# PSUM banks split three and five instead of four and four in a gated recurrent block

## What is computed

```python
rkv = x @ W_rkv + b_rkv ; r, k, v = split(rkv)
r = sigmoid(r) ; k = exp(k) ; kv = k * v
u1 = scan(lam, kv) ; u2 = scan(lam, k)            # y[t] = lam * y[t-1] + in[t], along the sequence
att = (u1 + gamma * kv) / (u2 + gamma * k + 1e-6) * r
z = layernorm(x + att @ W_o + b_o)
xr = mu_r * z + (1 - mu_r) * z_prev ; xk = mu_k * z + (1 - mu_k) * z_prev
out = layernorm(z + sigmoid(xr @ W_r) * (square(relu(xk @ W_k)) @ W_v))
```

## Time and profile before

| | |
|---|---|
| median of 3 runs | 2562.32 us (2560.85 to 2562.44) |
| the profiled execution | 2561.6 us, of it span 2559.8 us |
| mean granted TensorE clock | 0.992 of full speed |
| TensorE matmul busy | 2511.2 us, 98% of the span |
| VectorE, ScalarE, GpSimd busy | 79%, 50%, 48% |
| DMA | mean 43 GB/s |

### The profile page before, as it was taken

The page is one execution under the profiler, slowest core; times in us unless marked ns, Lnnn a source line. Parts: engine busy times, 40 slices in busy tenths (PEclk is TensorE's granted clock), DMA queues, the critical chain, the costliest instruction groups (busy, mean ns, idle before and its releaser), DMA issues.

```text
span 2559.8 us, 32879 instructions
## 1 busy us (share of the span) xinstructions
PE 2511.2 (98%) x11268; PEld 2076.2 (81%) x11268; DVE 2020.1 (79%) x2698; ACT 1269.4 (50%) x2159; POOL 1221.5 (48%) x1102
## 2 busy tenths in 40 slices
PE   6999999999999999999999999999999999999996
PEld 4888888888888888888888888888888888888885
DVE  8878888778787787877787887878877888777772
ACT  4444455454554444554445554545544455545454
POOL 4454454445454545544454535455444545454552
PEclk8999999999999999999999999999999999999998
DMA  4011111011100111101111111111011111111100
GB/s 160 17 50 50 33 50 34 34 51 50 34 34 35 49 50 33 50 34 34 50 50 34 38 35 45 50 35 49 34 34 50 50 35 40 36 41 50 41 30 21
DMA packets 57784, 110.63 MB, mean 43 GB/s; under 512 B 7040, under 2 KB 7040, under 8 KB 57088
## 3 DMA queue, kind: packets, MB, share of 16 engines
q1 hardware_dynamic: 57600, 108.31, 12.5%
HBM read 74.73 MB, written 33.55 MB: 42 GB/s over the span
## 4 chain that ended last, share of the span: by engine, by line
PE 96%; DVE 1%; issue 1%; ACT 1%; POOL 1%; DMA 0%; ACTq 0%; SPq 0%; POOLq 0%; DVEq 0%
PE bankB L835 13%; PE bankA L825 13%; PE bankA L827 13%; PE bankA L826 13%; PE bankB L837 13%; PE bankB L836 13%; PE bankB L877 5%; PE bankB L878 5%; PE bankB L879 5%; PE bankB L856 2%; DVE x_lo L626 0%; DVE gate L667 0%; DVE att_f L678 0%; DMA x_f<-in_xT 0%; DVE gate L670 0%
## 5 line engine op out<-in xcount | busy, mean ns | idle before, releaser
L825 PE MATMUL bankA<-x_hi,wrkv_hi 128*128 128x512 f32 x1536 | 603.2, 393 | 18.8 <-DVE x_lo L626 18.8
L827 PE MATMUL bankA<-x_hi,wrkv_lo 128*128 128x512 f32 x1536 | 599.6, 390 | 0.0
L826 PE MATMUL bankA<-x_lo,wrkv_hi 128*128 128x512 f32 x1536 | 599.5, 390 | 0.0
L670 DVE RECIPROCAL gate<-gate 128x512 f32<-128x512 f32 x128 | 429.2, 3353 | 4.4
L320 POOL TENSOR_TENSOR att_f<-att_f,gate 128x512 f32<-128x512 f32 x128 | 214.4, 1675 | 319.8 <-DVE att_f L683 319.6
L825 PEld LDWEIGHTS bankA<-x_hi,wrkv_hi 128*128 128x128 f32 x1536 | 289.5, 189 | 80.6 <-issue 16.6
L827 PEld LDWEIGHTS bankA<-x_hi,wrkv_lo 128*128 128x128 f32 x1536 | 289.4, 188 | 60.7
L826 PEld LDWEIGHTS bankA<-x_lo,wrkv_hi 128*128 128x128 f32 x1536 | 289.7, 189 | 59.1
L344 POOL TENSOR_TENSOR xk_lo<-xk_f,xk_hi 128x512 fp32r<-128x512 f32 x128 | 173.8, 1387 | 263.8 <-ACT xk_hi L491 263.8
L348 POOL TENSOR_TENSOR xr_lo<-xr_f,xr_hi 128x1024 fp32r<-128x1024 f32 x64 | 179.4, 2804 | 225.3 <-ACT xr_hi L495 225.3
L329 POOL TENSOR_TENSOR ve<-mv,eps_ln 128x2 f32<-128x2 f32 x128 | 60.9, 476 | 458.9 <-DVE mv L696 455.1
(11 more groups left out here) (89 smaller groups left out, 5431.1 us busy)
## 6 DMA issues: line engine op xcount, KB each, us to landing
x_f<-in_xT SPq DMA_DIRECT2D x128, 256.0 KB, 4.0
y<-in_x SPq DMA_DIRECT2D x128, 256.0 KB, 2.7
out<-z SPq DMA_DIRECT2D x128, 256.0 KB, 2.1
wrkv_f<-in_w_rkv SPq DMA_DIRECT2D x3, 768.0 KB, 6.8
wo_f<-in_w_o SPq DMA_DIRECT2D x1, 1024.0 KB, 10.3
wr_f<-in_w_r SPq DMA_DIRECT2D x1, 1024.0 KB, 12.0
wk_f<-in_w_k SPq DMA_DIRECT2D x1, 1024.0 KB, 13.9
wv_f<-in_w_v SPq DMA_DIRECT2D x1, 1024.0 KB, 15.9
```

The source lines that it names most:

```text
L670: dve.reciprocal(gate[:, c % 2], gate[:, c % 2]).then_inc(rec_made, 1)
L825: pe.matmul(bank[:], w_hi, x_hi[:, h], start=(h == 0), stop=False)
L826: pe.matmul(bank[:], w_hi, x_lo[:, h], start=False, stop=False)
L827: last = pe.matmul(bank[:], w_lo, x_hi[:, h], start=False, stop=(h == NC - 1))
```

## The change

Three banks go to the projections and five to the other products. Projection n now uses `bankA[n % 3]`, so each of K, V and R has a bank of its own, and waits on what took projection n-3: the one of its own kind in the chunk before. Slot n of the other products uses `bankB[n % 5]` and waits on what took slot n-5. At the start of step 0 TensorE writes five `bankB` instead of four, one more matmul, and `begin_sum` waits for five there.

```diff
-NBANK = 4
+NA, NB = 3, 5
 ...
-            return bankB[slot_of(name, index) % NBANK]
+            return bankB[slot_of(name, index) % NB]
 ...
-            n = slot_of(name, index) - NBANK
+            n = slot_of(name, index) - NB
 ...
-                act.activation(key[:, c % 2], bankA[(3 * c) % NBANK][:], ACT.Exp, bias=b_sb[:, 0, c:c + 1])\
+                act.activation(key[:, c % 2], bankA[(3 * c) % NA][:], ACT.Exp, bias=b_sb[:, 0, c:c + 1])\
 ...
-                        dve.wait_ge(columns_written, NBANK)
+                        dve.wait_ge(columns_written, NB)
 ...
-                m = n - NBANK
+                m = n - NA
 ...
-                bank = bankA[n % NBANK]
+                bank = bankA[n % NA]
 ...
-                            pe.matmul(bankB[h][:], wrkv_hi[:, c, which, h], x_hi[:, h], start=True, stop=True)\
-                                .then_inc(columns_written, 1)
+                            for bank_b in (bankB[h:h + 1] if h < NC - 1 else bankB[h:]):
+                                pe.matmul(bank_b[:], wrkv_hi[:, c, which, h], x_hi[:, h], start=True, stop=True)\
+                                    .then_inc(columns_written, 1)
```

## The result

Slower. The median of four runs is 2590.53 us (2588.63 to 2591.35) against 2562.36 us before; the ratio is 1.0112 with a 95% interval of 1.0100 to 1.0124, so 28 us more. The forecast was 24.5 us more, 2586 us in a range from 2581 to 2591. The ratio times the median before is 2591.1 us: the result sits on the range's upper edge, by this figure just past it. Direction and place were right, the size was 4 us short.

A forecast was written before the change was run, and what follows sets the result against it. TensorE, full in the steady steps, was taken to bound the kernel. 24.3 us for K3's wait plus 0.2 us for step 0, on 2561.6 us, gave 2586 us, range 2581 to 2591.

The forecast's parts named there:

- TensorE is full, and each tenth is paid 31 times: Steady steps: matmuls and transposes fill 78.0 of 78.10 us, so each new tenth of waiting is paid 31 times.
- K3 and only K3 waits in the steady steps: Of twelve projections only K3 lacks room: `exp_key` 2 frees its bank 0.79 to 0.87 us late, mean 0.845.
- The term of 24.3 us: K3's wait in 31 steps: 0.845 + 0.05 signal delay - 0.11 made up = 0.785 us a step.
- Step 0, 0.2 us: Start of step 0: the fifth bank costs one more matmul, 0.23 us, counted as 0.2 us.
- V2's wait in step 0: In step 0 TensorE stands 2.3 us at V2 until V1 is taken; counted as nothing because covered.
- the very thing that was to cover step 0: TensorE's 15.6 us wait at step 0's end for VectorE's low parts, said to cover V2's and V3's waits.
- The last block, 0 us: Last block: the 0.7 us receptance wait goes, but the value products wait 1.9 + 0.7 us instead; gain 0.
- The rival with the clock: K3's wait makes the clock fall, about 1.7 us a step, 53 us more: 2639 us; chance 0.02.
- that row: The trace row cited against the clock rival: a 1.9 us stop near 2534 left the granted clock at 1.00.
- More lost downstream: Rival: third receptance product's wait grows 0.2 to 0.3 us a step, 6 to 9 us, some 2594 us; chance 0.07.
- not slower: Rival: `exp_key` 2 comes 0.8 us sooner, K3 doesn't wait, 2561.8 us; chance of within 0.2% was 0.05.
- The bounds: K3's loss per step: 0.67 us if the third receptance product gains time, 0.90 us if nothing is made up.

The follow-up runs named there:

- The wait alone: Kernel before, four and four banks, with TensorE at K3 waiting for `exp_key` 2 too: 2587.94 us, ratio 1.0106.
- The run with `exp_key` 2 latest: Changed kernel, three and five banks, with ScalarE doing `exp_key` 2 behind `exp_gate` 2 and its second pass: 2684.98 us, ratio 1.0483.

## Why the prediction was right or wrong, point by point

- **TensorE is full, and each tenth is paid 31 times: right.** The chain, the steady distance and three different lengths of the same wait say so.
- **K3 and only K3 waits in the steady steps: right.** The wait alone gives the steady loss, and moving `exp_key` 2 takes it away. K1's room is 3.4 to 4.3 us in steps 2 to 31, less than the prediction read for it, and enough.
- **The term of 24.3 us was too small, 25.9.** Its first part held: the load starts 0.052 us after `exp_key` 2, and the second matmul is 0.784 us late on the mean of 31 steps, where the sum had 0.785. The step that failed is that the sum stopped there. The next ten matmuls run 0.228 to 0.234 us apart instead of 0.227, another 0.04 us: K3 as a whole is 0.827 us late, and the transposes are 0.834 us further apart. The product of the earlier trace rows could not have told: followed to its end it is 0.01 us later than at its second matmul.
- **Step 0, 0.2 us: too small, about 0.9.** In five profiles with three banks A step 1 transposes at 96.4 to 97.2 us, mean 96.9; in five with four banks and the same start at 94.9 to 96.5, mean 95.9. (The run with `exp_key` 2 latest, also with three banks, is at 99.1 us and is left out of this; with it the first mean is 97.2.) V2's wait in step 0 was foreseen. K1's wait for `exp_key` 0 was not: the room was 0.26 us in the one profile read (`exp_key` 0 over at 17.66 us, load at 17.92), while over the profiles with this start `exp_key` 0 ends between 17.66 and 18.95 us. But that wait isn't the loss: two of the five profiles don't have it and transpose at 97.1 and 96.6 us. The loss shows at the end of VectorE's low parts of the next x, at 66.4 us on the mean against 65.7, the very thing that was to cover step 0. What delays them stays open.
- **The last block, 0 us: the step that failed most.** The sum took the last block over from before; it is 2.5 and 2.1 us longer in the two profiles of the change. That the value product would wait 1.9 + 0.7 us instead was right (2.8). But the clock was not asked about there: it was at half speed behind that wait, 1.6 us, and for longer at the first key product, 0.8 and 0.4 us. Why stays open. With four banks B and the two waits apart it was the same, 2.6 us; with five and no stop at K3, and with the stop but four banks A, it was nothing, each in one profile.
- **Together** 25.9 + 1.4 + 2.5 = 29.8 us in the first profile, against 29.75 measured; the medians, 28 and 29 us, are of executions whose start and end differ, so the split outside the steady steps holds for the profiles alone.
- **The rival with the clock:** not at K3, where 0.9 us is too short, as the earlier trace rows suggested. But it is real for a stop of 2.4 us, and it was at work in the last block, where the prediction cited that row against it.
- **More lost downstream, not slower:** neither. The third receptance product's wait stayed as it was.
- **The bounds** for a step, 0.67 and 0.90 us, held 0.834. The range was tight because the start and the end went into it with nearly nothing.

## What to carry to other kernels

When a buffer is taken from a group, don't ask how long its reader takes but where the reader's instruction stands in its engine's queue, and compare its end with the start of the next writer's first weight load, step by step; here 0.87 us out of 78 decided, and one moved line of the reader's queue gave nearly all of it back. Keep single stops of TensorE short: 1.74 us once a step cost only its length here, 2.40 us also cost the clock. A stretch that the change doesn't touch can still come out at another clock, so give it a term or a bound. A gain in the steady steps is only a gain if the last step's own chain can deliver it: look at what the final wait does.

## What the runs showed of the hardware

- A stop of TensorE cost its lateness less 0.06 to 0.09 us as long as the clock held (loads 0.90, 0.96 and 1.74 us late): 0.12 us was made up by the second matmul, and 0.02 to 0.04 us lost again over the next ten, which started 0.227 to 0.236 us apart.
- The clock held behind 31 of 31 stops with the load 1.74 us late, and fell to 1.2 GHz behind 28 of 31 with it 2.40 us late; each fall cost 1.6 us. In the last block it fell behind 2 of 8 waits of 1.8 or 1.9 us and 5 of 6 of 2.7 or 2.8 us, which doesn't settle whether the length did it.
- K3's load started 0.052 us after ScalarE's instruction ended where K3 waited for that semaphore alone, and 0.113 us after it with a second wait ahead of it, each in all 31 steps.
